# Moving constants, weight halves, row sums and transposes to other steps in a two-layer mixture-of-experts kernel

## What is computed

```
# layer 0: W0[condition] acts on the 64 rows of a batch; 8 experts of rank 16
y = einsum('bct,bcd->bdt', x, weights[condition])
w = top-2 gates of softmax(y @ router_w.T + router_b)
x = x + (h * w) expanded by Bm * 0.5,        h = y by A
# layer 1: one of 16 adapter matrices (1024 x 1024) per batch, a base matrix, 16 experts of rank 64
y = einsum('bij,bkj->bik', x, weight[adapter_ids])
out = y @ base_w.T + base_b + 0.5 * sum over the top-2 experts of gate * B[e] (A y)
x = x + out
```

## Time and profile before

| | |
|---|---|
| median of 3 runs | 1114.62 us (1110.53 to 1116.79) |
| profiled execution, own time | 1110.44 us |
| its span, first to last instruction | 1108.8 us |
| mean granted TensorE clock | 0.995 of full speed |
| PE busy | 1075.5 us, 97% of the span |
| DVE, ACT, POOL busy | 61%, 45%, 20% |

### The profile page before, as it was taken

How to read it: one execution, slowest core, us unless ns; L and a number is a source line. 1 busy time by engine, 2 the same in 40 slices (tenths; PEclk the granted TensorE clock), 3 DMA queues, 4 the chain that set the end, 5 groups by cost and what they waited for, 6 DMA issues and landing times.

```text
span 1108.8 us, 21632 instructions
## 1 busy us (share of the span) xinstructions
PE 1075.5 (97%) x5844; PEld 916.6 (83%) x5845; DVE 673.4 (61%) x1231; ACT 501.5 (45%) x1021; POOL 219.8 (20%) x354
## 2 busy tenths in 40 slices
PE   7989999999999999999999999999999999999998
PEld 7989878888887888888888877877777888888887
DVE  5778843755738457564546588545555466666666
ACT  1122123745638456564536642145555434443444
POOL 2211010110202011110101000155553322222220
PEclk9999999999999999999999999999999999999999
DMA  9678683673947648583677342279999999999996
GB/s 304 242 280 330 221 327 96 236 268 126 340 158 246 231 160 311 196 271 124 229 236 233 96 133 85 78 285 346 356 345 353 344 396 357 335 356 323 333 337 205
DMA packets 126125, 283.57 MB, mean 256 GB/s; under 512 B 28146, under 2 KB 35570, under 8 KB 124146
## 3 DMA queue, kind: packets, MB, share of 16 engines
q1 hardware_dynamic: 96592, 180.59, 46.1%
q0 software_dynamic: 29216, 102.25, 26.4%
q10 hardware_dynamic: 258, 0.01, 0.0%
HBM read 181.50 MB, written 101.29 MB: 255 GB/s over the span
## 4 chain that ended last, share of the span: by engine, by line
PE 77%; DMA 7%; DVE 7%; ACT 3%; SPq 3%; issue 2%; DVEq 0%; ACTq 0%
PE psum L1562 17%; PE psum L1564 16%; PE psum L1563 16%; PE psum L1686 4%; PE psum L1573 4%; DMA xp<-act_scratch 3%; PE psum L1809 3%; PE psum L1810 3%; PE psum L1678 3%; PE psum L1704 2%; PE psum L1706 2%; PE psum L1687 2%; PE psum L1818 1%; SPq L548 1%; ACT w L896 1%
## 5 line engine op out<-in xcount | busy, mean ns | idle before, releaser
L1562 PE MATMUL psum<-base_hi,xp_hi 128*128 128x512 f32 (+3 forms) x520 | 204.3, 393 | 4.4 <-DVE xp_lo L1276 4.2
L1563 PE MATMUL psum<-base_lo,xp_hi 128*128 128x512 f32 (+3 forms) x520 | 198.9, 383 | 0.0
L1564 PE MATMUL psum<-base_hi,xp_lo 128*128 128x512 f32 (+3 forms) x520 | 198.7, 382 | 0.0
L1562 PE MATMUL psum<-w,xp_hi 128*128 128x512 f32 x448 | 181.2, 404 | 0.0
L1564 PE MATMUL psum<-w,xp_lo 128*128 128x512 f32 x448 | 176.8, 395 | 0.0
L1563 PE MATMUL psum<-w,xp_hi 128*128 128x512 f32 x448 | 176.6, 394 | 0.0
L699 POOL DMA_DIRECT2D raw<-w1T x112 | 59.2, 528 | 414.8 <-DVE w L1141 393.4
L1141 DVE TENSOR_TENSOR w<-raw,w 128x1024 fp32r<-128x1024 f32 x112 | 132.2, 1220 | 11.5 <-ACT w L830 8.5
L877 ACT ACTIVATE xp_hi<-xp 128x256 fp32r<-128x256 f32 x124 | 51.2, 416 | 170.3 <-PE psum L1564 158.1
L1562 PEld LDWEIGHTS psum<-base_hi,xp_hi 128*128 128x128 f32 x520 | 98.1, 189 | 27.7 <-DVE xp_lo L1276 5.4
L1276 DVE TENSOR_TENSOR xp_lo<-xp,xp_hi 128x256 fp32r<-128x256 f32 x124 | 51.7, 424 | 108.5 <-ACT xp_hi L877 107.9
(11 more groups left out here) (293 smaller groups left out, 1957.8 us busy)
## 6 DMA issues: line engine op xcount, KB each, us to landing
raw<-w1T POOLq DMA_DIRECT2D x120, 512.0 KB, 6.8
delta_scratch<-dl SPq DMA_DIRECT2D x80, 512.0 KB, 4.1
xp<-act_scratch SPq DMA_DIRECT2D x74, 256.0 KB, 3.3
act_scratch<-yT SPq DMA_DIRECT2D x72, 256.0 KB, 2.5
act_scratch<-x1g SPq DMA_DIRECT2D x16, 1024.0 KB, 5.2
x1t<-act_scratch SPq DMA_DIRECT2D x64, 256.0 KB, 4.8
out<-x1t SPq DMA_DIRECT2D x62, 256.0 KB, 5.4
xg<-xT SPq DMA_DIRECT2D x15, 1024.0 KB, 9.2
```

Of the source, the lines that this page charges most:

```text
L1562: mm(out, a_hi, b_hi, start=start, stop=False, skip_group_check=True)
L1563: mm(out, a_hi, b_lo, start=False, stop=False, skip_group_check=True)
L1564: return mm(out, a_lo, b_hi, start=False, stop=stop, skip_group_check=True)
```

## The change

Six places in which work stands at another step of its engine's list; no arithmetic is added or removed.

- DVE: `second_layer_constants` is cut in two. `sorting_constants` stands ahead of `add_x` in step n = 1 and `rank_constants` (two subtractions into `q2`) ahead of it in step n = 2. Of the three register loads one stands ahead of `add_x` in n = 2 and two in n = 3.
- PE: two register loads move from the adapter loop's head to step n = 6, between `keep_going(8)` and `turn_h0(7)`.
- ACT and DVE: at an adapter's last pair the turned y comes after one chunk of the next adapter, not after two.
- ACT: `expert_high(6)` and `(7)` move from ahead of tile 2's quarters to behind the second and the fourth.
- PE: `row_sums(0..5)` follow parts 5, 7, ..., 15 of tile 6 and `row_sums(6..7)` parts 1 and 3 of tile 7 (before: all eight behind parts 1, 3, ..., 15 of tile 6).
- PE: in the last stage `turn_out` follows parts 7 and 11 (before: 5 and 9), but for i = 1, where it stays at 9 and 13.

```
-                w_chunks(range(2))
+                w_chunks(range(1))
                 y_turned(j)
-                w_chunks(range(2, KC // 2))
+                w_chunks(range(1, KC // 2))
...
-            expert_high(6)
-            expert_high(7)
             for t in range(2, FIRST + 1):
                 for q in range(4):
...
                     y_high(t, q)
+                    if t == 2 and q % 2 == 1:
+                        expert_high(6 + q // 2)
...
-            def second_layer_constants():
+            def sorting_constants():
...
+            def rank_constants():
+                dve.wait_ge(const_split_hi, 3)
...
+                if n == 1:
+                    sorting_constants()
+                if n == 2:
+                    rank_constants()
+                    dve.wait_ge(table_ready, 1)
+                    used = w_used(dve)
+                if n == 3:
+                    total = start_of(dve, used)
+                    one = alone(dve, 0)
                 if n == NS - 2:
                     gates0(n + 1)
                 add_x(2 * n, 0)
                 add_x(2 * n, 1)
-                if n == 1:
-                    dve.wait_ge(const_split_hi, 3)
-                    second_layer_constants()
-                if n == 2:
-                    dve.wait_ge(table_ready, 1)
-                    used = w_used(dve)
-                    total = start_of(dve, used)
-                    one = alone(dve, 0)
...
-                low_chunks(range(2))
+                low_chunks(range(1))
...
-                low_chunks(range(2, KC // 2))
+                low_chunks(range(1, KC // 2))
...
                     keep_going(8)
+                    pe.wait_ge(table_ready, 1)
+                    used = w_used(pe)
+                    total = start_of(pe, used)
                     turn_h0(n + 1)
...
-            pe.wait_ge(table_ready, 1)
...
-            used = w_used(pe)
-            total = start_of(pe, used)
...
-                    if t == FIRST - 2 and n % 2 == 1:
-                        row_sums(n // 2)
+                    if t == FIRST - 2 and n % 2 == 1 and n > 3:
+                        row_sums((n - 5) // 2)
+                    if t == FIRST - 1 and n in (1, 3):
+                        row_sums(6 + n // 2)
...
-                    at = 9 if i == 1 else 5
+                    at = 9 if i == 1 else 7
```

More of the change, by code:

```diff
@@ L1644, in two_groups @@
                     z_of(2 * n + 4, 1)
+                return (used, total) if n == NS - 2 else None
             pe.wait_ge(ident_done, 2)
@@ L1665, in _ @@
             for n in range(NS):
-                two_groups(n)
+                counts = two_groups(n)
+                if n == NS - 2:
+                    used, total = counts
             keep_going(8)
-            pe.wait_ge(table_ready, 1)
             def turn(v):
```

## The result

The changed kernel takes 1097.27 us (median of 4 runs, 1095.64 to 1098.22). The kernel before takes 1112.57 us in the 4 runs that stand beside them (1110.49 to 1116.79). The ratio is 0.9847, with a 95% interval of 0.9808 to 0.9886: 1.5% faster. The profiled executions took 1110.44 and 1097.85 us, spans 1108.8 and 1096.3.

What follows compares the result with a forecast made beforehand. PE, busy 97% of the span, was taken to bound the kernel, so only its waits and low clock could be won. Terms of 11.4 us off 1110.4 gave 1099.0, raised for spread to 1101.5 us, range 1095 to 1108.

Steps and rivals of the forecast that it cites:

- constants, loads on DVE: Layer 0: work moved into DVE's idle time, so PE's waits of 1.69 and 1.98 us go; 3.7 us gained.
- register loads on PE: Adapter loop's head: two loads moved away remove nearly all of PE's 1.68 us wait; 1.6 us gained.
- adapters: One adapter pair: between 1.0 us gained and 2.4 lost through three waits and a later low clock; 0.7 us lost.
- experts' halves: Tile 2: quarters made ahead of ACT's expert halves remove PE's 1.37 us wait; 1.4 us gained.
- row sums: First row sum, four parts later: 2.6 us of the wait for hot_b and 1.5 of low clock go; 4.1 us.
- last stage: Later transposes in the last stage: transfers set the mixed tiles' times, so 1.34 us is won once; 1.3 us.
- gathers' slack of 0.6 us: Gathers behind the row sums: they land 3.6 us later, leaving 0.6 of 3.2 us; full queues would cost 1 to 2.
- somewhat more than half of the 4.2: Added to 1099.0 us, as the median lay 4.2 above the profiled execution and part may be low clock: 1101.5 us.
- the last stage follows PE: Rival, last stage: nearly all its waits go, 3.8 us, and the median nears the quickest execution; 1096.5 us, chance 0.13.
- Waits are handed on: Rival: adapter pair costs 2.4 us, gathers 1.5, clock falls behind another wait; 6.7 us left, 1106 us, chance 0.18.
- The ring rival: Rival, last stage: later transposes delay each next mixed tile by 1.34 us, 22.8 over 17 tiles; 1127 us, chance 0.04.

Runs made afterwards that it cites:

- e1: Kernel before with only DVE's layer 0 edit (constants and register loads moved to other steps): 1116.66 us in one run, kernel before 1119.67 on that chip.
- e2: Kernel before with only PE's two register loads moved from the adapter loop's head to the seventh pair: 1113.32 us in one run, kernel before 1119.67 there.
- e3: Kernel before with only one chunk of the next adapter, not two, ahead of the turned y: 1121.71 us in one run, kernel before 1119.67 there.
- e10: Changed kernel with only the adapters' edit undone on ACT and DVE: 1095.52 us in five runs, ratio 0.9847 to the kernel before.
- e8: Kernel before with only ACT's two expert halves moved behind quarters of tile 2: 1112.60 us in one run.
- e4: Kernel before with only the row sums moved four parts later: 1110.27 us in one run, kernel before 1119.67 on that chip.
- e6: Changed kernel with the last stage's transposes back behind part 5: 1099.23 us.
- e9: Kernel before with ten filler matmuls in PE's wait for the first row sum: 1110.48 us in twelve runs against 1113.9, ratio 0.9972.
- e5: Changed kernel again, unedited: 1097.77 us in six runs against 1112.95 for the kernel before, ratio 0.9844.
- e7: Changed kernel with the last stage's transposes behind parts 9, 12 and 15: 1097.32 us.
- e11: Changed kernel with another order on ACT and DVE for an adapter of one single pair: 1095.07 us in five runs, ratio 0.984 to the kernel before.

## Why the prediction came out right, and where it was off

It said 1101.5 us, 1095 to 1108, faster with 0.85. The time is 1097.27, within the range, and the gain was real. By its own steps:

| step | said | in the two profiles | by itself |
|---|---|---|---|
| constants, loads on DVE | 3.7 | 3.4 | 3.3 (e1) |
| register loads on PE | 1.6 | 1.6 | 1.5 (e2) |
| adapters | -0.7 | -0.7 | 0.0 (e3, e10) |
| experts' halves | 1.4 | 6.6 with the next | 1.9 (e8) |
| row sums | 4.1 | | 4.7 (e4) |
| last stage | 1.3 | 2.0 | 1.5 by medians to 3.4 by profiles (e6) |

**Where the mechanism was right.** The constants fit under PE's expansions, and step 3 gave nothing back. The loads were PE's wait at the loop head: it is gone whole, and 1.57 us with it. The size of one load was misread, though. The prediction took 0.97 us, a third of 2.90, and held that the trace has none by itself on PE. It has (L398 is `w_used`, L401 `start_of`, L406 `look_up`, which `alone` uses; ns, least, median and most). In the kernel before:

```profile
L398 PEldq TENSOR_LOAD <-table x1: 502/502/502, 140.1 to 140.1; - x1
L401 PEldq TENSOR_LOAD <-table x1: 911/911/911, 141.1 to 141.1; - x1
L406 SPq TENSOR_LOAD <-table x144: 262/269/286, 151.5 to 625.9; - x144
L406 DVEq TENSOR_LOAD <-table x37: 301/313/1487, 68.4 to 609.7; - x37
```

DVE's three took 0.56, 0.34 and 1.49 us before and 0.56, 0.32 and 0.31 after the change. So DVE's two loads in step 3 held it for less than the 1.94 us foreseen. The Trainium skill (DMA: Bandwidth & Descriptors, Latency and other measured facts) names about 600 ns as the least time of one; the trace does not agree, with 144 records of 0.26 to 0.29 us on SP, and the measurement decides. The gathers' slack of 0.6 us was enough. The row sums needed both parts of their term, the wait and the clock behind it: 2.6 and 1.5 were said, and e8 gives 3.3 and 1.4; e9 shows the second part by itself. That the transfers set the size in the last stage is not shown: the two profiles and e6's median give 2.0 and 1.5 us, the profiles taken together 3.4, near the 3.8 of a stage that follows PE. The Trainium skill (DMA: Bandwidth & Descriptors, Where 436 GB/s comes from) puts the limit of a core at HBM at about 358 GB/s; 359 to 368 GB/s were measured over those 130 us. The lower of these agree with it, but e10's 368 is above it, with PE busy throughout, so by the measurement 361 GB/s was not yet the most that the stage can move.

**The step that was right by accident.** The adapters' -0.7 matched the two profiles and is not an effect. Both profiles had a low stretch of 6.8 us; in the one of after it began 3 us behind the end of the first wait, in the one of before 1 us. The chain of reasoning to a loss was not borne out over twelve profiles (39.60 and 39.65); of its three waits two came (1.05 and 2.08 us), the third was 0.19 us in e3 and none in the profile of after, and how long the clock stays low differs by execution, with either order.

**The step that was off.** "Part of the spread may be further low stretches of the clock behind the same waits, which go too, so I add somewhat more than half of the 4.2": the first half of that sentence is what the runs show, and the number goes the wrong way. If the low stretches behind the removed waits go, the changed kernel's median has little to lie above its own quick execution by, and nothing should have been added. It lies 0.6 below the profiled one. The terms gave 12.9 us instead of 11.4, which makes 1097.5 out of 1110.4: that is the median to 0.3 us. Of the forecast's miss of 4.2 us, 2.5 are the amount added and 1.5 the terms. The kernel before lies above its profiled execution by more, and so the gain by medians, 15.3 us, is larger than the sum read in one pair of profiles.

**Where the other 2.5 us may be.** The profile of before has a mean clock of 0.995, as high as any of the eleven runs of the same kernel beside e5, whose median is 0.992. Behind the wait of 1.98 us the clock fell in three of six profiles, for 1.6 us each. Behind the 2.69 us it fell in four of five (before, e1, e2, e3; not e8), and those four have a mean B of 104.0 us, 2.6 above the profiled execution of before. The last stage has a share as well, by the 3.4 us there against the 2.0 in the one pair. How the 2.5 us divide is open. The prediction read "a wait of 1.98 us is not" followed by a low clock from one profile. That was this one execution's luck, not a rule.

**Of the rivals**, "the last stage follows PE" gave the time nearest to the result (1096.5). Its term of 3.8 is neither shown nor excluded: waits of 1.9, 2.0, 0 and 1.3 us are left with the transposes at 7, where it says 0.1, and L fell by 2.0 in the two profiles and 3.4 over all. "Waits are handed on" found its place (the adapter pair) without its price. The ring rival's 1.34 us per tile fell: 17 tiles would have made 22.8 us. A weak form of it is open, in e7.

## What to carry to other kernels

A wait of PE near 2 us or more is to be priced as the wait plus a chance of a low clock behind it, and the chance can't be read from one profile: look at the same wait in several. Two shorter waits close together can go with it too: in e2 PE was busy 1.44 of the 3.3 us ahead of the low stretch at the experts, around waits of 1.27 and 0.68 us. Where such a wait can't be removed, matmuls on a free bank in it can be worth having (some 3 us here). Edits of 1 us are measured between two landmarks around them in several profiles, not by the time of the run, and one pair of profiles can confirm a forecast that is not true.

## What the runs showed of the hardware

- How long the clock stays low behind one and the same wait varies: 0, 3.3, 13.4 or 16.8 us behind the 2.69 us at `hot_b` (e8; before and e2; e1; e3). B went from 98.0 (with 1.9 us of other gain in it) to 107.5 us.
- At the adapter pair, where PE waits 2.19 us or 1.05 and 2.08 us, the clock fell in all twelve profiles, for 3.4 us in six and 6.8 us in six. In e11, with no wait above 1.1 us there, it stayed at 1.00. In the last stage it fell behind a wait of 2.91 us (e8) and not behind one of 2.43 (e9).
- On the chip of e1 to e4 PE, ACT and POOL all stood still within 5 us at the experts' start, up to 2.2 us each; the other nine profiles, with 142.0 to 143.7 us for the experts against 145.7 to 148.7, don't show it. The trace names no releaser. It is open.
- The start scatters too: the first turned gates stood at 25.6 us in e10 and at 33.1 in e7, behind waits for the first x. That is in every run's time and in none of the terms.
